# A state-space block whose x, z and gate products are made from rounded parts, with their weights split in the block before

## The chip, the core and the metric

The kernel runs on one core of a Trainium2 chip. The core has five engines that run at the same time and meet only at semaphores: TensorE (PE; its weight loads are shown apart as PEld), VectorE (DVE), ScalarE (ACT), GpSimd (POOL) and SyncE (SP, which here only issues DMAs). The metric is the device time of one execution in microseconds (us), and a lower one is better. Before the change three runs took 1208.8, 1215.4 and 1216.16 us, with a median of 1215.4 us.

## The reference, cut to what matters

The whole program is a cross-attention, then a block that mixes a state-space branch, a self-attention branch and a first mixture of experts, then a second mixture of experts. The change is in the state-space branch and in what surrounds it:

```python
def ssm(x, Win, cw, cb, Wout):
    xz = x @ Win
    xs, z = jnp.split(xz, 2, axis=-1)
    xt = jnp.swapaxes(xs, 1, 2)
    y = jax.lax.conv_general_dilated(xt, cw, window_strides=(1,), padding=[(3, 0)], ..., feature_group_count=D) + cb[None, :, None]
    xc = jax.nn.silu(jnp.swapaxes(y, 1, 2))
    return xc * jax.nn.sigmoid(z) @ Wout
...
normed = layernorm(x, ln1_g, ln1_b)
r = normed @ Wr + br
alpha = jax.nn.sigmoid(r[..., 0:1])
ssm_out = ssm(normed, Win_ssm, conv_w, conv_b, Wout_ssm)
attn_out = gated_attention(normed, Wqkv, Wout, Wgate)     # ... * sigmoid(normed @ Wgate)
blended = ls1 * ((1 - alpha) * ssm_out + alpha * attn_out)
```

There are 2048 tokens (64 sequences of 32) with 256 channels, all in float32. The convolution has four taps along the sequence and works on each channel alone.

## The kernel before, in words

The program is a row of blocks. At a block's end all engines meet before the next block begins. Three blocks matter here.

**The merge block** (`merge_phase`, from L826) makes the input of the state-space branch. PE multiplies the attention output by Wo in eight pairs of 128-token tiles (`mg_xo`, L909). DVE adds each product to the residual (`add`, L951) and takes its statistics (`measure`, L956). After the fifth pair and after the last one it turns the statistics into scales (`scales(0)` and `scales(1)`, L963 to L970), for which ACT takes a square root (`root`, L1003). Then ACT and DVE normalise, PE turns the tiles to channels on partitions (`mg_tp`, L920) and ACT stores them as `nT` (L1012). DVE also normalises `xin`, and POOL adds that to `base` in DRAM by DMA (L895). SP writes `base` first. The loads of the state-space weights (`load_early`, seven DMAs, L70) are issued by SP behind the first of those writes, and the first write waits for the first two sums.

**The state-space block** (`state_space_phase`, from L1048) handles the tokens in eight steps of 256. In a step:

- PE multiplies float32 operands: x (`ss_xb`) and z (`ss_zb`, both L1116), four matmuls each with 256 columns, then the gates and r (`ss_gb`, L1125), four with 258 columns, and then the output of the step before (`ss_ob`, L1106), four more. The trace shows each float32 matmul as two instructions.
- ACT copies x out of PSUM into the padded tile `ss_xp` (L1160) and makes three sigmoids: of z (`ss_sz`, L1163), of the convolution (`ss_sy`, L1165) and of the gates (into `xs_oT`, L1167). A small one for `ss_beta` follows (L1171).
- DVE makes the convolution in `ss_y` with two tensor_scalar (L1198) and six scalar_tensor_tensor (L1201), one per tap and half of the channels, each behind the one before. Then it adds the bias of r (L1205, which waits for the gates' sigmoid) and adds the output of the step before (L1187).
- POOL copies the step's tokens to `ss_nS` for the gates' products (L1138) and makes the two multiplications y * sz (`ss_yz`, L1142) and yz * sy (`ss_gT`, L1146).

`ss_y`, `ss_sz` and `ss_xp` have one buffer each, so the next step's convolution waits for this step's `ss_gT`. SP issues the loads of the self-attention weights and of all experts (24 DMAs of 512 KB, L2817 and L2819) in this block.

**The self-attention block** follows. Its SP has nothing to do.

A rounded operand (`F32R`) occurs elsewhere: in the cross-attention block a product is made from a rounded part and a rest for each operand, as three matmuls into one PSUM tile, each shown as one instruction in the trace (L489 to L491, and L473 to L477 with 256 columns).

## Time and profile before

| what | us |
|---|---|
| median of three runs (lowest, highest) | 1215.4 (1208.8, 1216.16) |
| time of the profiled execution | 1215.3 |
| its span, from the first to the last instruction | 1213.5 |
| merge block, from its first instructions to the start of the next block | 493.5 to 524.0 |
| state-space block, from its start to its last DVE instruction | 524.1 to 586.1 |
| self-attention block | 586.4 to about 691 |

The profiled execution lies 1.8 us above its own span, and its time is within 0.1 us of the median. Over the whole span PE is busy for 89%, DVE for 64%, ACT for 53% and POOL for 66%, and the mean granted clock of TensorE is 0.944 of full speed. These shares are averages over blocks with different limits. What a change in one block is worth is read in that block: from the windows (busy time of each engine in a stretch, with the granted clock) and from the timeline (the instructions of one engine in order, with the idle time before them and what ended it).

### The profile page before, as it was taken

Reading aid. Unit: us, or ns where it says so; the run is one execution under the profiler, and the core shown is the slowest. Engines: PE = TensorE matmul, PEld = TensorE weight load, DVE = VectorE, ACT = ScalarE, POOL = GpSimd, SP = SyncE. Lnnn points to the kernel's source line nnn. Section 1 sums busy time; section 2 is a strip of 40 time slices with the busy share of each in tenths; the row PEclk is TensorE's granted clock in tenths of the full one; section 3 lists DMA queues with packets and bytes.
Section 4 is the critical chain, followed back from the end, with each engine's and each line's share of the span. In section 5 each row is a group of like instructions: output and inputs, shape, how many; then the busy total and the mean of one; then the engine's idle time right before and its main releaser. Section 6 shows DMA issues by size and latency. Waiting matters only on the chain. (4 is left out here: it accounts for less than half of the span.)

```text
span 1213.5 us, 27572 instructions
## 1 busy us (share of the span) xinstructions
PE 1083.2 (89%) x8144; PEld 975.0 (80%) x8145; DVE 779.4 (64%) x2339; ACT 648.8 (53%) x1500; POOL 803.5 (66%) x839
## 2 busy tenths in 40 slices
PE   5999999999999999889799953899999733999998
PEld 3799999999999999768577742788888632899897
DVE  7566666666666666655456568976666566655663
ACT  3556556565555564253467746666666442554451
POOL 2587787777777777034678741777768403799895
PEclk9899999999999999789899985999999965999999
DMA  5211111211211111288000050133332257645610
GB/s 151 69 55 52 56 52 53 71 54 54 70 54 56 52 54 41 104 236 285 1 1 0 0 127 27 32 53 52 52 52 48 36 152 232 188 112 116 164 36 10
DMA packets 72147, 94.27 MB, mean 78 GB/s; under 512 B 14828, under 2 KB 52160, under 8 KB 72096
## 3 DMA queue, kind: packets, MB, share of 16 engines
q1 hardware_dynamic: 53584, 73.00, 18.8%
q0 software_dynamic: 16032, 20.62, 10.4%
q8 instruction: 26, 0.43, 0.1%
q10 hardware_dynamic: 2480, 0.03, 0.1%
q14 instruction: 25, 0.20, 0.1%
HBM read 73.69 MB, written 22.18 MB: 79 GB/s over the span
## 5 line engine op out<-in xcount | busy, mean ns | idle before, releaser
L1912 POOL DMA_INDIRECT e_x<-rows,source x71 | 75.5, 1064 | 103.0 <-DMA rows<-weight 41.1
L122 POOL TENSOR_TENSOR xa_qbd<-qs,xw_c_mask8s 128x512 fp32r<-128x512 f32 x128 | 131.5, 1048 | 6.9 <-POOLq L133 3.8
L511 PE MATMUL xa_ob<-xa_v,xa_pT 128*128 128x65 f32 x1024 | 135.1, 276 | 0.2 <-DVE xa_pT L702 0.2
L632 ACT ACTIVATE xa_kT<-xa_kvp,xw_bk 128x258 fp32r<-128x258 f32 x128 | 60.9, 476 | 130.4 <-PE xa_kvp L465 123.1
L649 ACT ACTIVATE xa_pr<-xa_pr,xa_nm 128x257 f32<-128x257 f32 x256 | 109.6, 499 | 35.1 <-DVE xa_nm L698 35.0
L511 PEld LDWEIGHTS xa_ob<-xa_v,xa_pT 128*128 128x128 f32 x1024 | 126.5, 194 | 0.3 <-DVE xa_pT L702 0.3
L691 DVE TENSOR_SCALAR_CACHE_REDUCE xa_pr<-xa_sc 128x257 f32<-128x257 f32 x256 | 98.0, 420 | 25.0 <-PE xa_sc L491 25.0
L594 POOL TENSOR_TENSOR xa_ol<-xa_om,xa_tl 128x256 f32<-128x256 f32 x64 | 47.1, 736 | 80.7 <-DVE xa_rinv L719 80.6
L1917 POOL DMA_INDIRECT base<-e_y,place x39 | 74.2, 1902 | 36.3 <-DVE e_y L2200 21.8
L2579 PE MATMUL e_hb<-e_xTs,e_w1s 128*128 128x512 f32 x384 | 91.4, 398 | 1.9 <-issue 1.9
L2633 ACT ACTIVATE e_h<-e_hb,rc_F_b 128x512 f32<-128x512 f32 x64 | 44.0, 688 | 90.4 <-PE e_hb L2579 90.4
L702 DVE TENSOR_SCALAR xa_pT<-xa_ptp 128x512 f32<-128x512 f32 x128 | 87.6, 684 | 7.0 <-PE xa_ptp L500 3.2
L2595 PE MATMUL e_yb<-e_w2s,e_hTs 128*128 128x256 f32 x768 | 89.5, 278 | 0.0
L2595 PEld LDWEIGHTS e_yb<-e_w2s,e_hTs 128*128 128x128 f32 x768 | 88.2, 188 | 0.1
L711 DVE TENSOR_TENSOR xa_total<-xa_ob,xa_plast 128x4 f32<-128x4 f32 x64 | 10.3, 162 | 120.9 <-PE xa_ob L511 120.9
L2579 PEld LDWEIGHTS e_hb<-e_xTs,e_w1s 128*128 128x128 f32 x384 | 73.0, 192 | 18.0 <-issue 2.3
L127 POOL TENSOR_TENSOR xa_cs<-xa_ctx,xa_cs 128x514 fp32r<-128x514 f32 x64 | 82.7, 1292 | 6.1 <-ACT xa_cs L643 6.1
L1367 POOL TENSOR_TENSOR xs_oT<-sa_qkT,aw_c_mask 128x512 f32<-128x512 f32 x64 | 65.0, 1047 | 23.4 <-ACT sa_qkT L1410 23.4
L500 PE MATMUL xa_ptp<-xw_c_ident,xa_pr 128*128 128x128 f32 x512 | 77.3, 274 | 1.9 <-DVE xa_pT L702 1.9
L489 PE MATMUL xa_sc<-xa_kT,xa_qbd 128*128 128x258 f32 x256 | 78.2, 305 | 0.0
L490 PE MATMUL xa_sc<-xa_kT,xa_qbd 128*128 128x258 f32 x256 | 72.5, 283 | 0.0
L491 PE MATMUL xa_sc<-xa_kT,xa_qbd 128*128 128x258 f32 x256 | 72.5, 283 | 0.0
(362 smaller groups left out, 3287.6 us busy)
## 6 DMA issues: line engine op xcount, KB each, us to landing
e_w<-in_F_W SPq DMA_DIRECT2D x16, 1024.0 KB, 8.1
w<-in_W SPq DMA_DIRECT2D x24, 512.0 KB, 9.4
xa_ctx<-in_ctxT SPq DMA_DIRECT2D x32, 257.0 KB, 3.1
xa_ctx<-in_ctxT SPq DMA_DIRECT2D x64, 128.5 KB, 3.1
xa_vb<-vlx SPq DMA_DIRECT2D x64, 128.0 KB
rows<-xs_oT SPq DMA_DIRECT2D x8, 512.0 KB, 4.5
xs_oT<-in_x SPq DMA_DIRECT2D x4, 512.0 KB, 5.2
base<-xs_oT SPq DMA_DIRECT2D x4, 512.0 KB, 3.3
```

What stands on the lines that cost most here:

```text
L122: pool.tensor_tensor(dst, src, msk, ALU.mult).then_inc(o["q_ready"], 1)
L127: pool.tensor_tensor(o["cs"][:, par, 1, :, 0:S], o["ctx"][:, slot, :, par, :], o["cs"][:, par, 0, :, 0:S], ALU.subtract).then_inc(o["cr_re ...
L489: pe.matmul(out, qbd[:, par, 0, g, :], kT[:, par, 0, h, :], start=True, stop=False)
L500: mm = pe.transpose(ptp[:, c:c + P], pr[:, par, g, P * t:P * t + P], ident[:])
L511: mm = pe.matmul(ob[:, 65 * g:65 * g + 65], pT[:, par, g, t, :], v[:, vs, t, g, :], start=(g == 0 and t == 0), stop=(g == G - 1 and t == 1 ...
L649: act.activation(pr[:, par, g, :], pr[:, par, g, :], ACT.Exp, bias=nm[:, par, g:g + 1], scale=-1.0).then_inc(exp_ready, 1)
L691: dve.tensor_scalar(pr[:, par, g, :], sc[:, g, 0:S], CLAMP, None, ALU.min, ALU.min, accum_out=mx[:, par, g:g + 1]).then_inc(clip_ready, 1)
L702: dve.tensor_scalar(pT[:, par, 2 * h:2 * h + 2].rearrange("p g t c -> p (g t c)"), ptp[:], 1.0, None, ALU.min).then_inc(pT_ready, 1)
L1912: return pool.indirect_dma_start(out=out, out_offset=None, in_=rows, in_offset=bass.IndirectOffsetOnAxis(ap=index, axis=0))
L1917: return pool.indirect_dma_start(out=out, out_offset=bass.IndirectOffsetOnAxis(ap=index, axis=0), in_=rows, in_offset=None, compute_op=ALU ...
L2579: mm = pe.matmul(hb[:, f % HB, :], w1s[:, a, k, P * f:P * f + P], xTs[:, b, k, :], start=(n == 0), stop=(n == 5))
L2595: mm = pe.matmul(yb[:, s % 2, 0:D], hTs[:, a, f, P * s:P * s + P], w2s[:, par, b, f, :], start=(f == 0 and (a, b) == (0, 0)), stop=(f == M ...
```

## The change

The x, z and gate products are made from rounded parts. Each operand is split into a rounded high part and a rounded rest, and each float32 matmul becomes three matmuls (high by high, rest by high, high by rest) into the same PSUM tile: 12 instead of 4 for x, for z and for the gates. The output product stays as it was.

- The weights are split in the merge block: ACT makes the high parts (two instructions, `split_high`), DVE the rests (three subtractions, `split_low`, after the sums 3, 5 and 6). For this SP issues the state-space weights' loads at the start of the merge block.
- The tokens are split in the state-space block: ACT makes the high part of the next step at the start of a step, and POOL the rest (a subtraction in place of its copy). The rest of step 0 is made by DVE.
- `ss_y`, `ss_sz` and `ss_xp` get two buffers each.
- The gates' sigmoid goes ahead of the convolution's on ACT. On DVE the addition of r's bias goes into the middle of the convolution. POOL's first multiplication waits for the convolution and no longer for its sigmoid.
- The parts lie where `w2`, the experts' output weights, will lie, so the eight loads of `w2` move from the state-space block to the self-attention block.
- Steps 6 and 7 are written out and no longer in the loop.

```diff
@@ merge_phase @@
         def _(sp):
+            load_early(sp)
             for i in range(NG):
                 sp.wait_ge(x1_ready, 2 * i + 2)
                 sp.dma_start(base[:, GT * i:GT * i + GT, :], ...).then_inc(base_written[i], 16)
-                if i == 0:
-                    load_early(sp)
...
             for s in range(2, NS2):
                 add(s)
                 measure(s - 1)
+                if s in (3, 5, 6):
+                    split_low(dve, (3, 5, 6).index(s))
...
             act.activation(first[:], g1[:, 0:1], ACT.Sqrt)
+            split_high(act)
             root(0)
@@ new functions @@
+def high_state_space_weights(act, w, parts):
+    act.wait_ge(w.loaded, w.total)
+    for a, b in ((w["Wzx"], parts["zx"]), (w["Wgr"], parts["gr"])):
+        act.activation(b[:, 0], a[:], ACT.Copy).then_inc(parts["high"], 1)
+def rest_of_state_space_weights(dve, w, parts, n):
+    dve.wait_ge(parts["high"], 1 + n // 2)
...
@@ state_space_phase, tensor @@
+            pe.wait_ge(parts["low"], 3)
...
+                pe.wait_ge(parts["nh_ready"], s + 1)
...
-                        for k in range(2):
-                            mm = pe.matmul(bank[:, h, :], wzx[:, k, o + P * h:o + P * h + P], src[k],
+                        for n, (k, a, b) in enumerate(TERMS):
+                            if bank is xb and h == 0 and n == 4:
+                                ... pe.wait_ge(parts["nl_ready"], s)
+                            mm = pe.matmul(bank[:, h, :], wzx[:, a, k, o + P * h:o + P * h + P], nS[:, par, b, k, :],
@@ gpsimd @@
+            def low_part(s, par):
+                pool.wait_ge(parts["nh_ready"], s + 1)
+                pool.tensor_tensor(nS[:, par, 1], nT[...], nS[:, par, 0], ALU.subtract).then_inc(parts["nl_ready"], 1)
...
-                pool.wait_ge(sy_ready, s + 1)
+                pool.wait_ge(conv, s * 8 + 8)
                 pool.wait_ge(z_stored, s + 1)
                 pool.wait_ge(gT_ready, s)
-                pool.tensor_tensor(yz[:], y[:], sz[:], ALU.mult).then_inc(yz_ready, 1)
+                pool.tensor_tensor(yz[:], y[:, par], sz[:, par], ALU.mult).then_inc(yz_ready, 1)
@@ vector @@
                 dve.wait_ge(x_stored, s + 1)
-                dve.wait_ge(gT_ready, s)
+                if not static(s) or s >= 2:
+                    dve.wait_ge(yz_ready, s - 1)
+                    dve.wait_ge(sy_ready, s - 1)
...
                 for n in range(4):
+                    if n == 2:
+                        dve.wait_ge(g_stored, s + 1)
+                        dve.tensor_tensor(r_all[...], gb[:, :, D:D + 2], ...).then_inc(r_stored, 1)
```

On DVE in the merge block, from the fourth sum (`mg_xo` added) to the sums after the first scales, the instructions stood like this before:

```order
L951 TENSOR_TENSOR xs_oT<-mg_xo,xs_oT 128x512
L956 BN_STATS mg_stats<-xs_oT 128x6 x2
L951 TENSOR_TENSOR xs_oT<-mg_xo,xs_oT 128x512
L956 BN_STATS mg_stats<-xs_oT 128x6 x2
L963 BN_AGGR mg_mv<-mg_stats 128x2 x8
```

and they stand like this now (the second piece is the end of the sums):

```order
L950 TENSOR_TENSOR xs_oT<-mg_xo,xs_oT 128x512
L955 BN_STATS mg_stats<-xs_oT 128x6 x2
L1074 TENSOR_TENSOR sw_zx_parts<-sw_Wzx,sw_zx_parts 128x512
L950 TENSOR_TENSOR xs_oT<-mg_xo,xs_oT 128x512
L955 BN_STATS mg_stats<-xs_oT 128x6 x2
L962 BN_AGGR mg_mv<-mg_stats 128x2 x8
...
L1074 TENSOR_TENSOR sw_zx_parts<-sw_Wzx,sw_zx_parts 128x512
L950 TENSOR_TENSOR xs_oT<-mg_xo,xs_oT 128x512
L955 BN_STATS mg_stats<-xs_oT 128x6 x2
L1076 TENSOR_TENSOR sw_gr_parts<-sw_Wgr,sw_gr_parts 128x516
```

One subtraction of the weights stands ahead of the first scales, and two more stand ahead of the second scales.

On DVE in the state-space block, one step (`ss_y` is the convolution, `r_all` the addition of r's bias, `nT_xb` the output of the step before) was:

```order
L1198 TENSOR_SCALAR ss_y<-ss_xp,sw_cw,sw_cb 128x256 x2
L1201 SCALAR_TENSOR_TENSOR ss_y<-ss_xp,sw_cw,ss_y 128x256 x6
L1205 TENSOR_TENSOR r_all<-ss_gb,sw_br 128x4
L1187 SCALAR_TENSOR_TENSOR nT_xb<-ss_ob,ss_beta,nT_xb 128x256 x2
L1088 UNCONDITIONAL_BRANCH
```

and is now:

```order
L1263 TENSOR_SCALAR ss_y<-ss_xp,sw_cw,sw_cb 128x256 x2
L1266 SCALAR_TENSOR_TENSOR ss_y<-ss_xp,sw_cw,ss_y 128x256 x2
L1257 TENSOR_TENSOR r_all<-ss_gb,sw_br 128x4
L1266 SCALAR_TENSOR_TENSOR ss_y<-ss_xp,sw_cw,ss_y 128x256 x4
L1245 SCALAR_TENSOR_TENSOR nT_xb<-ss_ob,ss_beta,nT_xb 128x256 x2
```

The addition of r's bias, which waits for the gates' sigmoid, now stands between the fourth and the fifth of the eight instructions of the convolution.

## Rows read from the trace of the kernel before

**Rows 1.** Windows (stretch, its length, busy us of each engine, granted clock, DMA share, GB/s).
```profile
core 0: us, PE busy (x) PEld busy (x) DVE busy (x) ACT busy (x) POOL busy (x), PEclk, DMA share, GB/s
524.00:527.60 3.60, 3.27 (x8) 2.69 (x9) 0.00 (x0) 0.00 (x0) 2.32 (x4) 0.53 1.04 190
527.60:586.10 58.50, 54.41 (x250) 46.83 (x248) 33.52 (x88) 21.33 (x41) 24.16 (x23) 1.00 0.76 252
586.10:691.00 104.90, 94.52 (x1005) 73.54 (x1006) 59.01 (x150) 71.41 (x238) 80.97 (x83) 0.95 0.00 1
```

**Rows 2.** Timeline of PE, early steps (start us, us, what, [idle before]).
```profile
524.33 3.49 PE L1116 MATMUL ss_xb<-nT_xb,sw_Wzx 128*128 128x256 f32 x8 [1.32 <-PEq L831]
...
537.66 1.89 PE L1106 MATMUL ss_ob<-sw_Wos,ss_gT 128*128 128x256 f32 x8
...
544.58 0.59 PE L1106 MATMUL ss_ob<-sw_Wos,ss_gT 128*128 128x256 f32 x2
```

**Rows 3.** Timeline of PE, last step.
```profile
574.02 1.24 PE L1116 MATMUL ss_xb<-nT_xb,sw_Wzx 128*128 x5
...
577.47 1.91 PE L1125 MATMUL ss_gb<-sw_Wgr,ss_nS 128*128 128x258 f32 x8
...
583.22 1.97 PE L1106 MATMUL ss_ob<-sw_Wos,ss_gT 128*128 128x256 f32 x8 [2.11 <-POOL ss_gT L1146]
```

**Rows 4.** Timelines of ACT, DVE and POOL, last step.
```profile
577.67 0.60 ACT L1163 ACTIVATE ss_sz<-ss_zb 128x512 f32<-128x512 f32 x1 [1.04 <-PE ss_zb L1116]
...
577.32 2.46 DVE L1201 SCALAR_TENSOR_TENSOR ss_y<-ss_xp,sw_cw,ss_y 128x256 f32<-128x256 f32 x6
581.08 0.16 DVE L1205 TENSOR_TENSOR r_all<-ss_gb,sw_br 128x4 f32 x1 [1.31 <-ACT xs_oT L1167]
...
585.23 0.87 DVE L1187 SCALAR_TENSOR_TENSOR nT_xb<-ss_ob,ss_beta,nT_xb 128x256 f32<-128x256 f32 x2 [2.92 <-PE ss_ob L1106]
...
580.52 1.27 POOL L1142 TENSOR_TENSOR ss_yz<-ss_y,ss_sz 128x512 f32<-128x512 f32 x1 [3.75 <-ACT ss_sy L1165]
581.86 1.26 POOL L1146 TENSOR_TENSOR ss_gT<-ss_yz,ss_sy 128x512 f32<-128x512 f32 x1
```

**Rows 5.** Timeline of PE in cross-attention: rounded products of 256 columns, then another product.
```profile
300.17 0.36 PE L473 MATMUL xa_kvp<-xa_wvs,xa_cs 128*128 128x256 f32 x1
300.37 0.28 PE L474 MATMUL xa_kvp<-xa_wvs,xa_cs 128*128 128x256 f32 x1
...
301.43 1.00 PE L511 MATMUL xa_ob<-xa_v,xa_pT 128*128 128x65 f32 x8
```

**Rows 6.** Timelines of DVE and ACT in the merge block.
```profile
506.10 0.74 DVE L956 BATCH_NORM_STATS2 mg_stats<-xs_oT 128x6 f32<-128x256 f32 x2
506.94 0.69 DVE L951 TENSOR_TENSOR xs_oT<-mg_xo,xs_oT 128x512 f32<-128x512 f32 x1
507.55 0.74 DVE L956 BATCH_NORM_STATS2 mg_stats<-xs_oT 128x6 f32<-128x256 f32 x2
...
509.28 0.22 ACT L1003 ACTIVATE mg_rt<-mg_ve 128x16 f32<-128x16 f32 x1 [14.24 <-DVE mg_ve L967]
```

**Rows 7.** The page's DMA issues: the last of the state-space weights.
```profile
sw_Wos<-in_Wos SPq DMA_DIRECT2D x1, 256.0 KB, 6.3
```

**Rows 8.** Groups by shape: splits made elsewhere (count | busy, mean ns | idle before).
```profile
L2737 DVE TENSOR_TENSOR e_hTs<-e_h,e_hTs 128x512 fp32r<-128x512 f32 x64 | 44.4, 694 | 2.2
...
L1938 ACT ACTIVATE e_w1h<-w 128x1024 fp32r<-128x1024 f32 x8 | 8.4, 1044 | 2.2 <-PEq L1745 2.2
...
L127 POOL TENSOR_TENSOR xa_cs<-xa_ctx,xa_cs 128x514 fp32r<-128x514 f32 x64 | 82.7, 1292 | 6.1 <-ACT xa_cs L643 6.1
```

**Rows 9.** Step 2: POOL's copy beside DVE's tensor_scalar; last, all 16 of those (min/median/max).
```profile
541.90 0.61 POOL L1138 COPY ss_nS<-nT_xb 128x512 f32 x1
...
542.07 0.92 DVE L1198 TENSOR_SCALAR ss_y<-ss_xp,sw_cw,sw_cb 128x256 f32<-128x256 f32 x2 [1.30 <-ACT ss_xp L1160]
...
L1198 DVE TENSOR_SCALAR ss_y<-ss_xp,sw_cw,sw_cb x16: 401/410/593, 528.7 to 577.0; 128x256 f32<-128x256 f32 x16
```

More of the change, by code:

```diff
@@ L1045, in state_space_weights, with state_space_parts, there, state_space_phase @@
     return w
[L1048 removed]
+def state_space_parts(m, place):
+    zx, gr, n = 2 * 2 * 2 * D, 2 * 2 * (D + 2), 2 * 2 * 2 * V2
+    def there(name, shape, at, dt):
+        return m.nc.alloc_sbuf_tensor_at(name, shape, dt, offset=place + 4 * at)
+    return {"zx": there("sw_zx_parts", [P, 2, 2, 2 * D], 0, F32R), "gr": there("sw_gr_parts", [P, 2, 2, D + 2], zx, F32R),
+            "nS": there("sw_n_parts", [P, 2, 2, 2, V2], zx + gr, F32R), "y": there("ss_y", [P, 2, 2, V2], zx + gr + n, F32),
+            "sz": there("ss_sz", [P, 2, 2, V2], zx + gr + n + 4 * V2, F32), "high": m.sem("sw_high"), "low": m.sem("sw_low"),
+            "nh_ready": m.sem("sw_nh_ready"), "nl_ready": m.sem("sw_nl_ready"),
+            "first_nl_ready": m.sem("sw_first_nl_ready")}
+def high_state_space_weights(act, w, parts):
[4 more added lines that the diff above has]
+    dve.wait_ge(parts["high"], 1 + n // 2)
+    if n < 2:
+        dve.tensor_tensor(parts["zx"][:, 1, n], w["Wzx"][:, n], parts["zx"][:, 0, n], ALU.subtract).then_inc(parts["low"], 1)
+    else:
+        dve.tensor_tensor(parts["gr"][:, 1], w["Wgr"][:], parts["gr"][:, 0], ALU.subtract).then_inc(parts["low"], 1)
+def state_space_phase(nc, w, parts, nT, xb_, sg, r_all, base_added, load_early):
     with ExitStack() as st:
         p = Mem(nc, st)
[L1053 to L1057 removed]
+        wos, cw, cb, br = [w[n] for n in ("Wos", "cw", "cb", "br")]
+        wzx, wgr, nS, y, sz = [parts[n] for n in ("zx", "gr", "nS", "y", "sz")]
+        xp = p.sb("ss_xp", [P, 2, 2, BS, L + 3])
         sy = p.sb("ss_sy", [P, 2, V2])
@@ L1084, in state_space_phase @@
         block = st.enter_context(nc.Block(no_gpsimd_drain=True))
+        TERMS = [(k, a, b) for a, b in ((0, 0), (1, 0), (0, 1)) for k in range(2)]
         def steps(eng, step):
@@ L1087, in steps, with static @@
                 step(s, s)
-            with eng.Fori(1, NS // 2) as i:
+            with eng.Fori(1, NS // 2 - 1) as i:
                 for j in range(2):
                     step(i * 2 + j, j)
+            for s in range(NS - 2, NS):
+                step(s, s % 2)
+        def static(s):
+            return isinstance(s, int)
         @block.sync
@@ L1110, in step @@
             def step(s, par):
-                src = [nT[:, k, bass.ds(s * V2, V2)] for k in range(2)]
+                pe.wait_ge(parts["nh_ready"], s + 1)
                 for bank, o, ready, stored in ((xb, 0, x_ready, x_stored), (zb, D, z_ready, z_stored)):
@@ L1122, in step @@
                 for t in range(2):
-                    for k in range(2):
-                        lhs = nS[:, par, k, P * t:P * t + P]
-                        mm = pe.matmul(gb[:, t, 0:D + 2], lhs, wgr[:, k, :], start=(k == 0), stop=(k == 1))
+                    for n, (k, a, b) in enumerate(TERMS):
+                        mm = pe.matmul(gb[:, t, 0:D + 2], nS[:, par, a, k, P * t:P * t + P], wgr[:, b, k, :],
+                                       start=(n == 0), stop=(n == 5))
                 mm.then_inc(g_ready, 1)
@@ L1290, in place_v, with _ @@
                         eng.tensor_copy(dst, src).then_inc(ready, 1)
+        @block.sync
+        def _(sp):
+            load_late(sp)
         @block.tensor
@@ L2811, in build_program @@
             w13 = m0.sb("w13", [P, E * 4, F1])
+            at_w2 = next_place(nc)
             w2 = m0.sb("w2", [P, E * 4, D])
@@ L2818, in load_experts, with load_output_weights @@
                                      io[name][e].rearrange("(k p) f -> p k f", p=P)).then_inc(w_loaded, 16)
+            def load_output_weights(sp):
+                for e in range(E):
                     sp.dma_start(w2[:, 4 * e:4 * e + 4, :],
```

76 lines of the change are left out of this document (44 added, 32 removed).

## The prediction, made before the changed kernel was run

> **What bounds the kernel now.** I read the windows first, since the change touches three blocks only. In the state-space block TensorE is busy for 54.41 of 58.50 us at the full granted clock of 1.00, after 3.6 us at 0.53 [rows 1]. Next comes TensorE's timeline: from one output product to the next it is 544.58 - 537.66 = 6.92 us, which is four groups of 1.73 us with no gap [rows 2]. So this block is bound by TensorE, and the reader should see that before looking at any other engine. VectorE (33.52 us busy), ScalarE (21.33) and POOL (24.16) have room there [rows 1]. The exception is the end: the last output product starts at 583.22 after 2.11 us of idle time that ends with POOL's second multiplication [rows 3]. There a chain decides: VectorE's convolution, a sigmoid, POOL's two multiplications, the product, VectorE's last addition, up to 585.23 + 0.87 = 586.10 [rows 4]. In the merge block VectorE's sums and statistics follow one another, and ScalarE sits idle for 14.24 us until the first scales need its square root [rows 6]. So in that block VectorE sets the end.
>
> **The change, part by part.** The sum is made against the profiled execution (span 1213.5 us, time 1215.3 us, which is within 0.1 us of the median).
>
> *Merge block.* Three subtractions of 128x512 (the last of 516) join VectorE's row. The nearest row, a rest of the same shape, lasts 0.69 us [rows 8]; the start of one instruction of this size to the next is 507.55 - 506.94 = 0.61 us [rows 6]. The first falls into a short wait: the statistics that start at 506.10 need about 0.66 us (their 0.74 less 0.08 of overlap), but the next sum starts only at 506.94, when its product is there. That saves about 0.15 us, so it costs 0.46. The other two cost 0.61 each. **+1.7 us**; the bounds are 0 (if ScalarE's own row of normalisations ended the block anyway) and 3 x 0.69 = 2.1. ScalarE's two high parts (one of 128x1024 at 1.04 us, one of half that) lie in its 14.24 us of idle time. They need the weights, whose loads SP now issues first: seven issues, and 6.3 us to land for the last [rows 7]. Even at 1 us per issue from 493.5 they are there at 507, before the square root at 509.28. If that cover failed, the root and all behind it would wait as long as the weights are late after about 507.5.
>
> *Opening of the state-space block.* TensorE now waits for ScalarE's high part of step 0. A ScalarE instruction of 128x512 takes 0.60 us [rows 4]: **+0.6**. VectorE's rest of 0.69 us hides behind the first four matmuls at the low clock, about 0.94 us. The first product starts at 524.33 + 1.7 + 0.6 = 526.63.
>
> *The steps.* A rounded product of 256 columns starts every (301.43 - 300.37) / 9 = 0.118 us, and the first behind a float32 product takes 0.20, so 0.08 more [rows 5]. I take this for 258 columns too. The 36 products of a step need 36 x 0.118 + 0.08 = 4.33 us instead of 5.19; the output stays at 1.73. A step is 6.06 us instead of 6.92. The Trainium skill, "TensorE: Matmul & The Clock Gate", Back-to-back issue gap, gives N/2.4 + 2.5 ns, which is 109 ns for 256 columns. By it a step would be 0.32 us shorter and the block some 2 us; the row carries a weight load per product, and I go by the row.
>
> *Step 0.* Before, the low clock lasted from 524.33 to 527.6 [rows 1, 2]. I keep those 3.27 us: 14 products at 0.236, then 22 at 0.118 = 2.6. Step 1 begins at 532.5.
>
> *The chain behind the gates.* The convolution's second half now waits for r, and that for the gates' sigmoid. From the end of the gates' products to the output product: 0.20 to ScalarE (577.47 to 577.67), 0.60 sigmoid, 0.36 for r (its 0.16 and an estimated 0.1 on each side), 4 x 0.41 = 1.64 for the four instructions (2.46 / 6 each), 0.08, then 1.34 and 1.36 for POOL up to TensorE's start [rows 3, 4]. Sum 5.6 us. From a step's gates to its output product TensorE has 1.73 + 4.33 = 6.06 us of other work, so the chain is hidden with 0.5 us to spare, except twice. After step 0 there is no output of an earlier step, so only 4.33 us cover it: output 0 starts at 532.5 + 5.6 = 538.1 and step 2 at 539.8. And at the end nothing covers it.
>
> *The sum.* Step 7 starts at 539.8 + 5 x 6.06 = 570.1. Its products end at 574.4, its output product starts at 580.0, VectorE's last addition starts 2.01 us later and takes 0.87 [rows 3, 4]: 582.9 instead of 586.1. **-3.2 us**: +2.3 ahead of the first product, -6.2 from there to the start of step 7, +0.7 in the end chain. The time is 1215.3 - 3.2 = **1212.1 us**.
>
> *Edits costed at nothing.* ScalarE gets one more instruction of 0.6 per step and POOL's copy of 0.61 becomes a subtraction of 1.29 [rows 8, 9]. POOL then has 1.34 + 1.36 + 1.29 = 4.0 of 6.06 us, and the subtraction stands behind a multiplication that is due 0.5 us later. The second buffers only take waits away. The eight loads of w2 go to a block with a DMA share of 0.00 for 104.9 us [rows 1]; 4.2 MB at the 252 GB/s of the block before are 17 us, and they are used after that block.
>
> **What the trace does not show** is VectorE at its two-input convolution while POOL works on SBUF. Before, the two took turns; now POOL's second multiplication and its subtraction run beside the next step's first half. The nearest row: one tensor_scalar took 0.593 instead of 0.40 us beside POOL's copy, with 0.44 us of overlap, and the copy kept its 0.61 [rows 9]. So VectorE lost 0.19 of 0.44, that is 43%. At that rate the first half (0.65 + 0.82 us) gets 0.65 longer. It could start 2.2 us after the step's start and must end by about 5.5, so it stays hidden. That is my value: 0. The other end is full exclusion, below. The Trainium skill, "SBUF — State Buffer", Two separate sides, says that VectorE with two SBUF inputs and a POOL instruction that reads SBUF lock each other out for the whole instruction. By that rule the sum is the first rival's and not -3.2. [...]
>
> **The rivals.**
>
> 1. *VectorE and POOL exclude each other: slower.* Then a new loop binds from one convolution's end to the next: 2.7 for two multiplications, 1.29 for the subtraction, 0.82 + 1.64 for six two-input instructions, 0.3 for r, in sum 6.75; with the two tensor_scalar (0.65) it is 7.4. I take 7.1, since the row shows that tensor_scalar is held too, but not for all of the time [rows 9]. The first convolution ends at 532.5 + 0.2 + 0.6 + 0.36 + 1.64 = 535.3; seven loops less the last step's missing subtraction give 535.3 + 49.7 - 1.3 = 583.7; then 2.8 for POOL and 2.9 for the product and the addition: 589.4, so +3.3 and **1218.6 us**. At 6.75 it is 1216.1, at 7.4 1220.7. The point from which the kernel becomes slower is a loop of 6.63 us. For it: [rows 9] show a stretch, and POOL and VectorE were never together on this work. Against it: the copy was not stretched and the loss was partial.
> 2. *The low clock lasts through step 0.* All 36 products at 0.236 make 8.5 instead of 5.9 us: +2.6, **1214.7 us**. For it: the products now come with a wait, and the clock has only just come up by 527.6 [rows 1]. Against it: TensorE has as little idle time as before.
> 3. *The inserted work is hidden.* If the merge block ends with ScalarE's row, -1.7 more: **1210.4 us**. Against it: ScalarE waits for VectorE's scales [rows 6].
> 4. *The change doesn't do what it says*, for example because the weights come late in the merge block or a sigmoid holds the convolution back: about 0, 1215.
>
> **How the numbers follow.** Chances: forecast 0.45, rival 1 0.30, rival 2 0.10, rival 3 0.07, rival 4 and others 0.08. The three runs shown differ by 7.4 us, so a median can lie some 3 us from the profiled time. The low end is rival 3 less that: 1207. The high end is rival 1 at its value: 1219. Gain and loss are both small; the likeliest case's own range is 1208.5 to 1215. A change of 1% is 12 us, about what separates a change from none here. No case reaches it, so I give 0.03 to faster, 0.94 to the same and 0.03 to slower.
>
> **What would show it.** In the profile after: three instructions of about 0.69 us on VectorE in the merge block and the first product near 526.6; 36 products at 0.118 in a step; a distance of 6.06 us between output products from the third on; output 0 preceded by about 1.3 us of idle time on TensorE that POOL ends; and the last addition ending near 583. It is wrong if the output products are 6.7 us or more apart, with idle time that POOL ends in each step and convolution instructions above 0.48 us; if the granted clock stays near 0.5 past 530; or if self-attention is longer than its 104.9 us.

## The result and the profile after the change

The changed kernel takes 1219.4 us (median of 10 runs, 1217.4 to 1223.9), the kernel before 1214.5 us in the same comparison. The ratio is 1.0058, with a 95% interval of 1.0042 to 1.0074: slower by half a per cent, where 1212.1 us and a small gain were forecast. The profiled execution after took 1219.2 us, its span is 1217.4 us.

Other blocks move by several us from run to run (cross-attention ended at 488.2 to 495.3 us over all kernels of this study), so the blocks that the change touches are compared by their own lengths, read from the timelines. The merge block is counted from VectorE's first instruction (`mg_same`) to the start of ScalarE's last store of a transposed tile:

| us | before | forecast | after |
|---|---|---|---|
| merge block | 29.45 | +1.7 | 31.23 (+1.8) |
| end of it to the first product | 1.29 | +0.6 | 2.00 (+0.7) |
| state-space block, first product to the end of the last addition | 61.77 | 56.3 | 63.95 (+2.2) |
| self-attention, from there to the same product (`sa_outb`, at 690.96 and 694.75) | 104.9 | 104.9 | 103.0 |

The first three rows add up to +4.7 us, and the medians differ by 4.9. Self-attention is no longer than before: over all thirteen kernels the same stretch lies between 103.0 and 104.9 us, so its -1.8 is scatter.

First the windows of the changed kernel, in the columns of [rows 1]: step 0 in two pieces, the rest of the block in three, and self-attention (a longer stretch of it than in the table).

```profile
core 0: us, PE busy (x) PEld busy (x) DVE busy (x) ACT busy (x) POOL busy (x), PEclk, DMA share, GB/s
526.80:530.40 3.60, 0.71 (x4) 0.54 (x4) 2.78 (x1) 1.15 (x2) 3.04 (x4) 0.80 1.05 188
530.40:536.70 6.30, 6.25 (x32) 6.25 (x33) 1.53 (x4) 2.49 (x3) 0.00 (x0) 0.57 1.07 234
536.70:581.40 44.70, 41.68 (x302) 39.23 (x300) 36.09 (x73) 19.08 (x41) 25.24 (x20) 1.00 0.55 204
581.40:587.30 5.90, 2.12 (x10) 1.44 (x8) 3.94 (x10) 1.32 (x3) 3.08 (x3) 0.97 0.00 0
587.30:591.80 4.50, 3.47 (x8) 2.52 (x8) 0.88 (x2) 0.00 (x0) 0.00 (x0) 0.66 0.00 0
591.80:697.00 105.20, 93.78 (x1042) 73.50 (x1043) 60.23 (x152) 72.09 (x240) 83.10 (x85) 0.98 0.13 41
```

The low clock is there twice: at 0.57 in most of step 0 and at 0.66 in the last output product. From 536.7 to 581.4 it is 1.00, yet TensorE isn't busy all of the time. Its timeline, which answers to [rows 2, 3], shows where:

```profile
527.77 0.71 PE L1157 MATMUL ss_xb<-sw_n_parts,sw_zx_parts 128*128 128x256 f32 x4 [2.03 <-ACT sw_n_parts L1205]
530.45 2.08 PE L1157 MATMUL ss_xb<-sw_n_parts,sw_zx_parts 128*128 128x256 f32 x8 [1.97 <-DVE sw_n_parts L1235]
...
536.74 1.56 PE L1157 MATMUL ss_xb<-sw_n_parts,sw_zx_parts 128*128 128x256 f32 x12
...
548.89 1.99 PE L1142 MATMUL ss_ob<-sw_Wos,ss_gT 128*128 128x256 f32 x8 [0.52 <-POOL ss_gT L1191]
...
555.67 1.99 PE L1142 MATMUL ss_ob<-sw_Wos,ss_gT 128*128 128x256 f32 x8 [0.55 <-POOL ss_gT L1191]
...
587.34 3.47 PE L1142 MATMUL ss_ob<-sw_Wos,ss_gT 128*128 128x256 f32 x8 [3.32 <-POOL ss_gT L1191]
```

There are three losses. In step 0, TensorE stops for 1.97 us after four products. From one output product to the next it is 6.46 to 6.78 us (6.78 between the two that are shown), with 0.2 to 0.55 us of idle time in front of each. And the last output product takes 3.47 us, where it took 1.97 before [rows 3].

Why TensorE stops in step 0 is seen on VectorE and POOL. Their timelines there:

```profile
527.62 2.78 DVE L1235 TENSOR_TENSOR sw_n_parts<-nT_xb,sw_n_parts 128x512 fp32r<-128x512 f32 x1 [1.80 <-ACT sw_n_parts L1205]
...
527.03 1.59 POOL L1195 TENSOR_TENSOR sw_Wos<-sw_Wos,mw_ls 128x512 f32<-128x512 f32 x1
528.26 1.57 POOL L1177 TENSOR_TENSOR sw_n_parts<-nT_xb,sw_n_parts 128x512 fp32r<-128x512 f32 x1
```

VectorE's subtraction, 0.69 us elsewhere [rows 8], is on record for 2.78 us. It ends at 530.40, when both of POOL's instructions are over. A duration in a profile can hold a wait that no semaphore shows.

The same in a steady step, where the timelines answer to [rows 9]:

```profile
559.29 1.29 POOL L1186 TENSOR_TENSOR ss_yz<-ss_y,ss_sz 128x512 f32<-128x512 f32 x1 [2.67 <-DVE ss_y L1266]
560.65 1.29 POOL L1191 TENSOR_TENSOR ss_gT<-ss_yz,ss_sy 128x512 f32<-128x512 f32 x1
561.90 1.32 POOL L1177 TENSOR_TENSOR sw_n_parts<-nT_xb,sw_n_parts 128x512 fp32r<-128x512 f32 x1
...
561.17 2.19 DVE L1263 TENSOR_SCALAR ss_y<-ss_xp,sw_cw,sw_cb 128x256 f32<-128x256 f32 x2 [1.18 <-ACT ss_xp L1213]
563.29 0.87 DVE L1266 SCALAR_TENSOR_TENSOR ss_y<-ss_xp,sw_cw,ss_y 128x256 f32<-128x256 f32 x2
...
564.16 1.66 DVE L1266 SCALAR_TENSOR_TENSOR ss_y<-ss_xp,sw_cw,ss_y 128x256 f32<-128x256 f32 x4
```

The pair of tensor_scalar takes 2.19 us. It ends at 563.36, 0.14 us after POOL's subtraction (561.90 + 1.32 = 563.22). Only then do the two-input instructions start, and they keep their normal time. All instructions of the convolution in one view (count: min/median/max ns); the second row answers to the last of [rows 9]:

```profile
L1266 DVE SCALAR_TENSOR_TENSOR ss_y<-ss_xp,sw_cw,ss_y x48: 468/473/481, 533.9 to 584.1; 128x256 f32<-128x256 f32 x48
L1263 DVE TENSOR_SCALAR ss_y<-ss_xp,sw_cw,sw_cb x16: 408/1166/1372, 533.3 to 580.7; 128x256 f32<-128x256 f32 x16
```

The median tensor_scalar went from 410 to 1166 ns; POOL's instructions kept their time (1.27 to 1.33 us, once 1.39). The trace has 13 of the 16 tensor_scalar at 0.9 us or more, and each of the 13 ends 0.15 or 0.16 us after an instruction of POOL. The two-input instructions, which the prediction asked about, never ran beside POOL here: when the long pair is over, POOL is done.

The merge block came out as forecast (+1.8 for +1.7). Its timelines, for [rows 6]:

```profile
508.00 0.67 DVE L1074 TENSOR_TENSOR sw_zx_parts<-sw_Wzx,sw_zx_parts 128x512 fp32r<-128x512 f32 x1
508.59 0.68 DVE L950 TENSOR_TENSOR xs_oT<-mg_xo,xs_oT 128x512 f32<-128x512 f32 x1
...
502.38 1.06 ACT L1067 ACTIVATE sw_zx_parts<-sw_Wzx 128x1024 fp32r<-128x1024 f32 x1 [6.39 <-DMA sw_Wos<-in_Wos]
503.34 0.62 ACT L1067 ACTIVATE sw_gr_parts<-sw_Wgr 128x516 fp32r<-128x516 f32 x1
...
510.92 0.21 ACT L1004 ACTIVATE mg_rt<-mg_ve 128x16 f32<-128x16 f32 x1 [6.96 <-DVE mg_ve L966]
```

Each inserted subtraction costs VectorE 0.59 us from start to start, and ScalarE's high parts end 7 us ahead of the square root.

### The profile page after: what moved, and what is told of

Read it like the earlier page. It is cut to its first block and busy times, and to the rows that moved or that the text cites. A ratio compares the mean times of both kernels' runs of the same rounds, so it can differ in the third digit from the quotient of the medians.

```text
span 1217.4 us, 27738 instructions
## 1 busy us (share of the span) xinstructions
PE 1077.1 (88%) x8240; PEld 972.9 (80%) x8241; DVE 793.1 (65%) x2343; ACT 652.9 (54%) x1510; POOL 806.8 (66%) x838
```

## The experiments

Eleven kernels were run, ten derived from the changed kernel and the last from the kernel before. The theory: a VectorE instruction whose inputs are all in SBUF does not run while a POOL instruction runs. The rivals: the sigmoid of the gates ahead of the convolution's holds the chain; TensorE needs more time for rounded products than was thought; POOL's third instruction is simply too much for POOL. "Block" is the state-space block of the table above, 63.95 us in the changed kernel (where an expectation says 63.84 or 56.84, it is the same length read from start times with one decimal), and "steps" are the distances from one output product to the next. For kernels that ran once the whole time tells little, since single times of one kernel lie up to 10 us apart (1206.4 to 1217.0 us for the kernel before in one comparison). e5, e8 and e9 were timed in several runs.

**e1: POOL waits for the first rest.** Only POOL's start is later:

```diff
             pool.wait_ge(w.loaded, w.total)
+            pool.wait_ge(parts["first_nl_ready"], 1)
             pool.tensor_tensor(wos[:], wos[:], ls1[:]..., ALU.mult).then_inc(wosl_ready, 1)
```

> The changed kernel with one more wait: POOL scales the output weights only after VectorE has made the rest of step 0. In the changed kernel that rest took 2.78 us, where the same shape takes 0.69 elsewhere, and POOL worked on SBUF all the time. Theory (POOL and VectorE shut each other out of SBUF): the rest takes about 0.7 us, TensorE's pause of 1.97 us behind its first four products is gone, and from the first product to the last addition the block takes 61 to 62 us instead of 63.95. Rival (VectorE's first instruction of a block is slow in itself, or waits for code): the rest stays at 2.8 us and the block at 64.

Measured: the block is 61.33 us. TensorE and VectorE in step 0:

```profile
523.63 2.24 PE L1157 MATMUL ss_xb<-sw_n_parts,sw_zx_parts 128*128 128x256 f32 x12 [2.03 <-ACT sw_n_parts L1206]
...
523.48 0.69 DVE L1236 TENSOR_TENSOR sw_n_parts<-nT_xb,sw_n_parts 128x512 fp32r<-128x512 f32 x1 [1.78 <-ACT sw_n_parts L1206]
```

The subtraction is back at 0.69 us, the pause is gone (12 products in one piece), and step 0 is 6.04 us. The steps after it stay at 6.47 to 6.75. So a wait placed on POOL gives 2.6 us back: 2.9 in step 0, less 0.3 in the last output product, which took 3.75 us here.

**e2: POOL makes no rests after step 0's.**

```diff
-                if not static(s) or s < NS - 1:
+                if static(s) and s == 0:
                     low_part(s + 1, 1 - par)
...
-                                else:
+                                elif static(s) and s == 1:
                                     pe.wait_ge(parts["nl_ready"], s)
```

> The changed kernel without POOL's subtraction from step 2 on: the products of the steps 2 to 7 read the rests of the steps 0 and 1, so those results are not the reference's. Theory (VectorE's first two instructions of the convolution are held while POOL works): only one of the two is still held, by POOL's second multiplication, so the two last about 1.3 us instead of 2.2 to 2.4, output products are 6.0 to 6.2 us apart instead of 6.7, and the block is some 3 us shorter than 63.95. Rival (the wait of the convolution's second half on the gates' sigmoid sets the step): the distance stays at 6.7 us. Rival (36 products and an output need more than 6.06 us on TensorE): it stays near 6.5 with no idle time on TensorE.

Measured: the block is 60.27 us, the steps are 5.97 to 6.09. The tensor_scalar and two output products:

```profile
L1263 DVE TENSOR_SCALAR ss_y<-ss_xp,sw_cw,sw_cb x16: 401/412/1500, 526.6 to 570.9; 128x256 f32<-128x256 f32 x16
```

```profile
553.41 1.89 PE L1142 MATMUL ss_ob<-sw_Wos,ss_gT 128*128 128x256 f32 x8
559.47 1.99 PE L1142 MATMUL ss_ob<-sw_Wos,ss_gT 128*128 128x256 f32 x8
```

No idle time is left in front of the output product. With the gates' sigmoid still ahead and the products unchanged, TensorE runs at 6.06 us per step on average, which is the forecast's step: both of those rivals fall. What this run can't tell is whether POOL's subtraction costs by holding VectorE or by its own 1.29 us in POOL's row.

**e3: the first taps read PSUM.** The two tensor_scalar read x where TensorE left it; POOL keeps all its work.

```diff
                     pe.wait_ge(stored, s)
+                    if bank is xb and not (static(s) and s == 0):
+                        pe.wait_ge(conv, s * 8 - 6)
...
-                            ins = dve.tensor_scalar(yv[:, h], src, tap, ...)
+                            ins = dve.tensor_scalar(yv[:, h], xb[:, h, :].rearrange("p (b q) -> p b q", q=L), tap, ...)
```

> The changed kernel, but the convolution's two tensor_scalar read x from PSUM (behind ScalarE's copy, as before), not from the padded tile in SBUF. Theory A (only what VectorE reads through SBUF is shut out, and its two-input instructions too): the two take 0.41 us each again, but the two-input instructions behind them are held by POOL's subtraction, so the step stays at 6.5 to 6.7 us. Theory B (the two-input instructions of this convolution are not held): they stay at 0.47 us, the step falls to 6.06 to 6.2 us and the block by 3 us. Rival (every VectorE instruction that writes SBUF is held while POOL works): the two stay at 1.0 to 1.3 us and the step at 6.7.

Measured: the block is 60.09 us, the steps are 6.07 to 6.44, less than theory A's 6.5 to 6.7.

```profile
L1268 DVE SCALAR_TENSOR_TENSOR ss_y<-ss_xp,sw_cw,ss_y x48: 468/476/1531, 530.1 to 577.6; 128x256 f32<-128x256 f32 x48
L1265 DVE TENSOR_SCALAR ss_y<-ss_xb,sw_cw,sw_cb x16: 535/541/547, 529.2 to 574.7; 128x256 f32<-128x256 f32 x16
```

No tensor_scalar is held any more: the slowest takes 547 ns, and 14 of the 16 ran beside POOL. POOL does the same three instructions per step as before, so its load alone was not the cause. But the next instruction in the row, a scalar_tensor_tensor with two SBUF inputs, now falls into POOL's subtraction, and up to 1531 ns stand where 473 is normal. The hold moved on by one instruction. Of the 3.9 us that the block gains, only some 2.4 come from the steps and the last chain; 1.5 are the last output product, which took 1.97 us here instead of 3.47, after 3.12 us of idle time.

**e4: both sigmoids in their old order.** The gates' sigmoid and r's addition go back behind the convolution's end.

```diff
+                act.wait_ge(conv, s * 8 + 8)
+                act.wait_ge(gT_ready, s)
+                act.activation(sy[:], y[:, par], ACT.Sigmoid).then_inc(sy_ready, 1)
                 act.wait_ge(g_ready, s + 1)
                 act.activation(sg[...], gb[:, :, 0:D], ACT.Sigmoid).then_inc(g_stored, 1)
-                act.wait_ge(conv, s * 8 + 8)
-                act.wait_ge(gT_ready, s)
-                act.activation(sy[:], y[:, par], ACT.Sigmoid).then_inc(sy_ready, 1)
```

> The changed kernel with ScalarE's sigmoids in the order of before (the convolution's ahead of the gates') and the addition of r's bias behind the whole convolution. Rival (that added wait sets the step): output products 6.06 us apart instead of 6.7 and the block 4 us shorter. Theory (POOL and VectorE take turns): VectorE's first two instructions stay at 1.0 to 1.3 us each, and the step only loses the 0.15 us of r's addition, 6.5 to 6.6 us; the end of the block is shorter by 1 to 1.5 us, since the last convolution does not wait for the gates.

Measured: the block is 62.58 us, the steps are 5.97, 6.38, 6.91, 7.06, 6.9, 6.69. VectorE's pair of tensor_scalar, and TensorE, which now waits at another place:

```profile
559.24 1.27 DVE L1258 TENSOR_SCALAR ss_y<-ss_xp,sw_cw,sw_cb 128x256 f32<-128x256 f32 x2 [1.00 <-ACT ss_xp L1213]
...
557.44 1.69 PE L1164 MATMUL ss_gb<-sw_gr_parts,sw_n_parts 128*128 128x258 f32 x12 [0.67 <-DVE r_all L1265]
```

The old order does not bring the forecast's 6.06 back. But the theory's expectation was wrong too: only one tensor_scalar of a step is held here (the median of the 16 is 412 ns), not both, and the end of the block is 0.2 us shorter, not 1 to 1.5. What the hold gives back is lost to another wait, since the gates' products now wait until r has been read. The six steps together last 39.9 us in both kernels. The block gains 1.4 us, of which 1.2 are step 1, where the new order has a price of its own. So e4 alone does not clear the new order; e2 and e8, which keep it and have steps of 6.06 and 5.97 us, do.

**e5: e1 and e3 together**, timed.

> Two earlier edits together: POOL scales the output weights only after VectorE's first rest, and the first two convolution instructions read x from PSUM. Theory (VectorE's instructions that read SBUF alone are held while POOL works, and TensorE pays for that once at step 0 and once per step): the two gains add. The first edit took 2.5 us off the block and the second 3.8, so the block is 63.84 - 2.5 - 3.8 = 57.5 us, the pause before the fifth product is gone, steps are 6.1 to 6.4 us, and the span is about 1211. Rival (both edits removed the same lost time, since a late start of step 0 only shifts the first steps): the block stays at 60 or above.

Measured: the block is 58.23 us (57.5 expected), the steps are 6.07 to 6.44. The kernel takes 1213.6 us against 1213.1, ratio 1.0011 (0.9987 to 1.0035). The two gains add, except 0.7 us, since the last output product is slow again.

```profile
576.95 2.86 PE L1142 MATMUL ss_ob<-sw_Wos,ss_gT 128*128 128x256 f32 x8 [3.14 <-POOL ss_gT L1193]
```

**e6: the weights' rests on POOL.**

```diff
         def _(pool):
+            for n in range(3):
+                split_low(pool, n)
             for i in range(NG):
...
-                if s in (3, 5, 6):
-                    split_low(dve, (3, 5, 6).index(s))
```

> The three subtractions for the weights' rests in the merge block are made by POOL, which is idle there for 31 us, and no longer by VectorE. POOL needs about 3 x 1.3 = 3.9 us for them. Theory (POOL holds VectorE only where VectorE reads SBUF alone): the additions (one input in PSUM) keep their 0.63 us; the bn_stats, which read SBUF, may be held for part of the 3.9 us. If nothing is held the merge block is 29.4 us as before the change (now 31.3); if all of POOL's time is lost to VectorE it is 33.3.

Measured: the merge block is 30.8 us, 0.4 less than in the changed kernel, and not 29.4. VectorE and POOL:

```profile
499.40 0.74 DVE L957 BATCH_NORM_STATS2 mg_stats<-xs_oT 128x6 f32<-128x256 f32 x2
500.06 3.19 DVE L944 COPY_PREDICATED xs_oT<-mg_bad,mean 128x512 f32<-128x512 uint32 x2
503.16 0.67 DVE L952 TENSOR_TENSOR xs_oT<-mg_xo,xs_oT 128x512 f32<-128x512 f32 x1
503.75 0.73 DVE L957 BATCH_NORM_STATS2 mg_stats<-xs_oT 128x6 f32<-128x256 f32 x2
...
499.70 2.96 POOL L1074 TENSOR_TENSOR sw_zx_parts<-sw_Wzx,sw_zx_parts 128x512 fp32r<-128x512 f32 x2 [12.02 <-ACT sw_zx_parts L1067]
502.63 1.74 POOL L1076 TENSOR_TENSOR sw_gr_parts<-sw_Wgr,sw_gr_parts 128x516 fp32r<-128x516 f32 x1
```

Beside POOL the sums (one input in PSUM) and the statistics (one input in SBUF) keep their times. The pair of predicated copies takes 3.19 us instead of 1.33. What VectorE saves, 3 x 0.6 = 1.8 us, it loses again in this pair (1.86); the remaining 0.4 is within the scatter of this block (30.7 to 31.2 us in the kernels that keep the subtractions on VectorE). POOL's work is also longer here, 2.96 us for two subtractions, where 2.51 is seen in e9 below.

**e7: filler products**, to keep TensorE busy in its two pauses.

```diff
                                 if static(s) and s == 0:
+                                    for _ in range(4):
+                                        for v in range(2):
+                                            pe.matmul(ob[:, v, :], wzx[:, 0, 0, 0:P], nS[:, 0, 0, 0, :], start=True, stop=True)
...
             steps(pe, step)
+            pe.wait_ge(x_stored, NS)
+            for _ in range(13):
+                for v in range(2):
+                    pe.matmul(xb[:, v, :], wzx[:, 0, 0, 0:P], nS[:, 0, 0, 0, :], start=True, stop=True)
             output(NS - 1, 1)
```

> Products whose result nobody reads are added on TensorE: 8 while it waits for the first rest in step 0, and 26 between the output product of step 6 and that of step 7. Nothing else is changed. Theory (the low clock of 530.4 to 536.7 and of the last output product comes from TensorE's idle time just before): step 0, now 8.97 us, becomes about 7.9, the last output product takes 1.97 instead of 3.47, and the block 61.2 instead of 63.8. Rival (the clock is low for another reason, such as the power of the rounded products): the clock stays at 0.57 after 530 and the last output product at 3.4 us or more, and the block stays at 63.8.

Measured: the block is 60.81 us (61.2 expected). Step 0 is 7.26 us instead of 8.97 (7.9 expected), and the last output product is back at 1.97:

```profile
579.04 1.97 PE L1142 MATMUL ss_ob<-sw_Wos,ss_gT 128*128 128x256 f32 x8 [0.33 <-issue]
```

Nothing but useless work was added, and 3.1 us came back. So 1.7 us of step 0 and 1.5 us at the end were the low clock after TensorE's idle time. The rival, that the clock is low for another reason, such as the rounded products themselves, falls: the fillers are rounded products too.

**e8: the whole convolution from PSUM**, timed. x stays in two PSUM banks by turns, ScalarE's copy is gone, and each tap adds only the columns it reaches.

```diff
-        xb = p.ps("ss_xb", [P, 2, V2])
+        xb = p.ps("ss_xb", [P, 2, 2, V2])
...
-                        src, tap = xp[:, par, h, :, 3 - n:3 - n + L], cw[:, h, 3 - n:4 - n]
+                        src = xb[:, par, h, :].rearrange("p (b q) -> p b q", q=L)[:, :, 0:L - n]
+                        dst, tap = yv[:, h, :, n:L], cw[:, h, 3 - n:4 - n]
```

> All eight convolution instructions read x from PSUM, in two banks by turns; ScalarE's copy of x to SBUF and POOL's memset are gone; POOL scales the output weights after the first rest. Each of VectorE's instructions then has one input in PSUM and one in SBUF. Theory (it is the reading of two SBUF inputs, or of SBUF alone, that POOL holds): no convolution instruction is above 0.6 us, steps are 6.06 us, and the block about 57. Rival (an instruction with one SBUF input beside the PSUM one is held just as well): one or two per step at 1.1 to 1.5 us, as the 1.531 us of the scalar_tensor_tensor seen when only the first two read PSUM, and the block stays at 57.5 to 60.

Measured: the block is 56.88 us and the steady steps are 5.97.

```profile
L1262 DVE SCALAR_TENSOR_TENSOR ss_y<-ss_xb,sw_cw,ss_y x48: 448/458/471, 525.6 to 571.3; 128x248 f32<-128x248 f32 x16, 128x240 f32<-128x240 f32 x16, 128x232 f32<-128x232 f32 x16
L1259 DVE TENSOR_SCALAR ss_y<-ss_xb,sw_cw,sw_cb x16: 534/536/545, 524.7 to 567.1; 128x256 f32<-128x256 f32 x16
```

Of 64 instructions the slowest takes 545 ns, with POOL's three instructions per step still there; 34 of the 64 ran beside one of them. One SBUF input beside one in PSUM is not held. The shorter steps do not come from that alone, since ScalarE's copy has left the chain as well; the durations show the hold by themselves. The kernel takes 1212.1 us against 1213.1, ratio 0.9993 (0.997 to 1.0015): no difference that can be told.

**e9: all of it**, timed (six runs). To e8 come the filler products at the end, and in the merge block POOL makes the rests and scales the output weights, timed to keep clear of the predicated copies and the small scale instructions:

```diff
         def _(pool):
+            pool.wait_ge(guarded, 10)
+            split_low(pool, 0)
+            split_low(pool, 1)
+            pool.wait_ge(shift_ready, 1)
+            split_low(pool, 2)
+            scale_wos(pool)
             for i in range(NG):
```

> The convolution from PSUM as before, and in the merge block POOL makes the three rests and scales the output weights, but only after VectorE's predicated copies are over (two rests then, the third and the scaling after the first shifts), and 26 filler products stand ahead of the last output product. Theory: the additions and statistics of the merge block read PSUM or a single SBUF input in a form that was not held (0.67 and 0.73 us beside POOL in the run with the rests on POOL), so the block loses the 3 x 0.61 us and comes back to 29.1 to 29.5; the state-space block was 56.84, less 1.4 for the last product at the full clock: 55.4. Against the kernel before that is 0 + 0.7 - 6.3 = -5.6 us, a ratio of 0.995. Rival (POOL's instructions hold the statistics or the small scale instructions): the merge block stays at 30.6 or more, and the ratio at 0.997 to 0.999.

Measured: 1207.1 us against 1215.3, ratio 0.9939 (0.9919 to 0.996): the one version whose time is clearly below that of the kernel before. The merge block is 29.5 us as in the kernel before, the state-space block 56.46. POOL in the merge block:

```profile
503.20 2.51 POOL L1078 TENSOR_TENSOR sw_zx_parts<-sw_Wzx,sw_zx_parts 128x512 fp32r<-128x512 f32 x2 [14.08 <-DVE xs_oT L948]
...
509.46 1.28 POOL L1080 TENSOR_TENSOR sw_gr_parts<-sw_Wgr,sw_gr_parts 128x516 fp32r<-128x516 f32 x1 [3.75 <-DVE mg_shift L975]
```

The block was expected at 55.4. The last product is at full clock, but step 0 took 7.01 us here and 6.15 in e8, which is 0.9 of the missing 1.1. By the blocks the difference is 0.1 + 0.6 - 5.3 = -4.6 us; the ratio says -7.4 (-9.8 to -4.9). The other 3 us lie in no block that was changed, and what they are stays open.

**e10: POOL's rest after the first taps.**

```diff
                 if not static(s) or s < NS - 1:
+                    if not static(s) or s >= 1:
+                        pool.wait_ge(conv, s * 8 + 4)
                     low_part(s + 1, 1 - par)
```

> One wait is added to the changed kernel: from step 1 on POOL makes the next step's rest only after the first four of a step's eight convolution instructions. It then works while VectorE waits for the gates. Theory (two tensor_scalar are held, one by POOL's second multiplication and one by its subtraction): only the first is still held, the pair falls from 2.2 to 1.3 us and the chain per step by about 0.9; the rest is ready some 1.3 us later, which is at about the fifth product of the next step. Steps 6.1 to 6.4 us, block 61.0 to 62.5 (now 63.84, with the pause of step 0 left in). Rival (the late rest becomes TensorE's wait): the idle time moves from before the output product into the first group of x products, ended by POOL's subtraction, and steps stay at 6.5 to 6.8.

Measured: the block is 64.63 us and the steps are 6.56 to 6.86. Worse than the changed kernel, so the expected 61.0 to 62.5 was wrong. VectorE, POOL and TensorE in a step:

```profile
560.05 1.25 DVE L1265 TENSOR_SCALAR ss_y<-ss_xp,sw_cw,sw_cb 128x256 f32<-128x256 f32 x2 [1.18 <-ACT ss_xp L1215]
...
562.12 2.69 DVE L1268 SCALAR_TENSOR_TENSOR ss_y<-ss_xp,sw_cw,ss_y 128x256 f32<-128x256 f32 x4
...
562.37 1.37 POOL L1177 TENSOR_TENSOR sw_n_parts<-nT_xb,sw_n_parts 128x512 fp32r<-128x512 f32 x1 [1.54 <-DVE ss_y L1268]
...
563.79 1.22 PE L1157 MATMUL ss_xb<-sw_n_parts,sw_zx_parts 128*128 128x256 f32 x8 [0.26 <-POOL sw_n_parts L1177]
```

The pair of tensor_scalar falls to 1.25 us, as the theory said. But VectorE does not wait for the gates in that place: its four two-input instructions are already running, and they take 2.69 us instead of 1.66. The hold moved again, and TensorE's idle time moved to the rest, as the rival said.

**e11: the kernel before, with a longer POOL.**

```diff
                 pool.tensor_copy(nS[:, par], nT[:, :, bass.ds(s * V2, V2)]).then_inc(nS_ready, 1)
+                pool.wait_ge(gT_ready, s)
+                pool.tensor_tensor(yz[:], nT[:, :, 0:V2], nT[:, :, V2:2 * V2], ALU.subtract).then_inc(extra, 1)
+                pool.wait_ge(extra, s + 1)
```

> The kernel before, with a subtraction of 128x512 that nobody needs added on POOL behind its copy in each step (1.29 us beside the copy's 0.61). Theory (a tensor_scalar that starts while POOL works ends about 0.15 us after POOL's instruction has ended): where only one of 16 took 0.593 us, one per step from step 2 on takes about 1.3, and never more. The reading of the prediction (VectorE loses 43% of the overlap): none above 0.40 + 0.43 x 1.3 = 0.75 us. TensorE bounds this kernel, so under both the steps stay at 6.92 and the block at 61.7.

Measured: the block is 70.0 us and the steps are 7.76. POOL, VectorE and TensorE:

```profile
560.28 0.61 POOL L1139 COPY ss_nS<-nT_xb 128x512 f32 x1
560.85 1.31 POOL L1141 TENSOR_TENSOR ss_yz<-nT_xb 128x512 f32<-128x512 f32 x1
...
560.44 1.87 DVE L1202 TENSOR_SCALAR ss_y<-ss_xp,sw_cw,sw_cb 128x256 f32<-128x256 f32 x2 [0.75 <-POOL ss_gT L1150]
...
560.94 2.01 PE L1126 MATMUL ss_gb<-sw_Wgr,ss_nS 128*128 128x258 f32 x8 [0.57 <-POOL ss_nS L1139]
```

Two things were expected. The longest tensor_scalar takes 1353 ns (view of all 16: min 408, median 595, max 1353), so the hold is right, and the 0.75 us that the prediction's reading allows is refuted. That the steps would stay at 6.92 was wrong: this kernel's loop (convolution, sigmoid, POOL's two multiplications, convolution) took about 6.5 us of each 6.93 (576.66 to 581.86 + 1.26 = 583.12 in the last step before), and the pair at 1.87 us instead of 0.74 made it the bound.

## Why the prediction was wrong

**The failed step: "That is my value: 0", for POOL beside VectorE.** The prediction took from [rows 9] that VectorE loses 43% of an overlap: 0.593 instead of 0.40 us, with 0.44 us of overlap. The same row says something else if one looks at when the instruction ended. POOL's copy ended at 541.90 + 0.61 = 542.51, the tensor_scalar at 542.07 + 0.593 = 542.66, 0.15 us later. The trace of the kernel before has two more that are longer than their like: 0.592 us from 535.31, beside a copy that ended at 535.75, and 0.447 us from 548.96, beside one that ended at 549.26. Both end 0.15 us after the copy, and the second lost only 0.04 us for 0.30 us of overlap, which is not 43%. In e11 it is 560.44 + 0.592 = 561.03 after a copy that ended at 560.89, again 0.15. In the changed kernel a held pair ends 0.15 or 0.16 us after POOL (550.07 after 549.91; 556.77 after 556.61). So it was a full wait whose cost was small only because the overlap was short: of 0.40 us about 0.25 pass beside POOL in any case. By these rows an overlap of 1.3 us costs about 1.0, not 0.56. The hold took 2.0 us in step 0 and 2.9 in the five steps after step 1, where the forecast had nothing.

The Trainium skill, "SBUF — State Buffer", section "SBUF: two separate sides", calls it an exclusive lock for the whole instruction, taken also by a VectorE operation in a two-port mode. The prediction used only that page's rule for two SBUF inputs. The Trainium skill, "VectorE: DVE Perf Modes", section "Mode 2×_2P — use both read ports for one tensor", counts a float32 tensor_scalar from SBUF among the two-port operations. The trace agrees: 0.41 us from SBUF and held, 0.54 us from PSUM and not held (e3).

**Rival 1 named the mechanism and nearly the loop.** Its lower end, 6.75 us, left the tensor_scalar out. Measured from one convolution's end to the next (552.51 to 559.21) it is 6.70: 0.08, then POOL's three instructions from 552.59 to 556.61, 0.16 until the held pair ends, and 2.44 for the six two-input instructions with r between. The pair is covered whole by the POOL instruction that holds it, except its last 0.16. The value taken, 7.1, was too high, and the rival's 1218.6 us came near the measured 1219.4 by luck: at the measured 6.70 its own sum gives 1215.8, and it priced nothing in step 0 or for the clock.

**"VectorE's rest of 0.69 us hides behind the first four matmuls": wrong.** It took 2.78 us, and TensorE stood still for 1.97. POOL's scaling of the output weights stood at the same place before the change and held nobody that mattered. The change put a two-input VectorE instruction beside it, with TensorE behind. The first four products were no cover of 0.94 us either: they ran at the full clock, 0.12 us apart, and took about 0.5 us. e1, which only keeps POOL away, takes 2.9 us off step 0, its share of the low clock included.

**Step 0 in 5.87 us: wrong, 8.97.** 2.0 us are that pause, 1.1 the low clock. The forecast let the low clock begin with the first product and end 3.27 us later. In the trace it fell in the pause, and from 530.45 to 535.75 the products are 0.21 us apart. (e7 gains 1.7, more than 1.1, since with its fillers two thirds of the low stretch lie in the pause itself.) Without the pause step 0 is 6.04 (e1), 6.21 (e5) and 6.15 (e8), but 7.01 in e9. So the term was right to 0.3 us in three of four kernels, in part by luck: the low spacing was taken as 0.236 us, where 0.213 is measured, and in e1 the first products ran at the full clock. Rival 2 asked 8.5 us for the 36 products; besides the pause they took 7.0, halfway between it and the forecast.

**A step of 6.06 us: right as TensorE's need, not as the step.** e2 shows 6.06 on average and e8 5.97. The five distances from the start of step 2 to that of step 7 hold 576.96 - 543.75 = 33.21 us against 30.3, so +2.9.

**The end chain: 5.6 us forecast, 5.97 measured** (from the gates' last product, 579.95 + 12 x 0.118 = 581.37, to 587.34); the last pair of tensor_scalar took 1.70 us beside a multiplication. Then 1.5 us more in the last output product, which TensorE ran at 0.66 after 3.32 us of idle time. The prediction had seen that idle time (5.6 us less the output product of step 6) and put no clock on it.

**The account.** 56.3 forecast for the block; +3.1 in step 0, -0.3 in step 1 with its chain, +2.9 in five steps, +1.95 at the end: 63.95, as measured. The held instructions of VectorE account for some 5 us of it and the low clock for 2.6. The merge block (+1.8 for 1.7) and the opening (+0.7 for 0.6) were right, as were the loads of w2, which cost nothing. The merge blocks of the other kernels that keep the three subtractions on VectorE were 30.7 to 31.2, so a part of the 1.8 is scatter.

## What to carry to other kernels

Work moved to POOL is not free because POOL is idle: ask which VectorE instructions with all inputs in SBUF start while it runs, and who waits for them (the statistics were such a form and were not held, e6). When an instruction is longer than its like, compare its end with the end of the other engine's instruction before making a rate out of it; a lag that stays the same (here 0.15 us) means a full wait. To escape, give VectorE an operand in PSUM, or make POOL wait; moving the conflict to another VectorE instruction only moves the loss.

## What the runs showed of the hardware

- Held beside a POOL instruction: tensor_scalar of 128x256 from SBUF to SBUF (0.41 to 1.51 us, the longest in e4), tensor_tensor of 128x512 with both inputs in SBUF (0.69 to 2.9), scalar_tensor_tensor of 128x256 with both in SBUF (0.47 to 1.53), and a predicated copy (a pair of 128x512 from 1.33 to 3.19). Not held: the same two convolution forms with x in PSUM (at most 0.548), additions with one input in PSUM (0.67), statistics of one SBUF input (0.73 a pair).
- A waiting instruction can miss a turn. The rest of step 0 started before POOL's second instruction did, and still ended only after it (530.40, POOL at 528.26 + 1.57 = 529.83).
- After about 3.1 us of idle time TensorE's next output product took 1.97 us in one run (e3, 3.12 us) and 2.86 in another (e5, 3.14); after 3.3 to 3.5 us it took 3.2 to 3.75. Filler products were worth 3.1 us here.
- How long the low clock of step 0 lasts differs by run: the step took 6.04, 6.15, 6.21 and 7.01 us in four kernels whose TensorE work there is the same (e1, e8, e5, e9), and its products were 0.21 us apart until 4.6, 4.2, 4.2 and 5.9 us after the first. Why is open.
